# A vision tower's attention steps: both heads' scores issued together, and one row maximum for the two

## What is computed

```python
# xt: 257 rows of the image (normed) and 196 shared rows: 453 keys; 12 heads of width 16
qkv = (xt @ W_qkv).reshape(B, N1, 3, H, Dh)
attn = softmax(einsum('bhqd,bhkd->bhqk', q, k) * Dh ** -0.5)
out = einsum('bhqk,bhkd->bhqd', attn, v)[..., :257 rows]
h = h + out @ W_proj + b_proj
```

## Time and profile before

| | us |
|---|---|
| median of 3 runs | 716.21 (713.61 to 717.03) |
| the profiled execution | 714.55, with a span of 712.7 |
| TensorE busy in the span | 608.6 (85%) |
| VectorE | 281.4 (39%) |
| ScalarE | 202.5 (28%) |
| GpSimd | 144.8 (20%) |
| straight scores L660, 192 passes of 96 products | 62.5, mean 590 ns |
| maxima L879, 96 operations | 55.9, mean 623 ns |
| turned products L678, 384 passes | 65.9, mean 399 ns |
| exponentials L843, 48 operations | 49.1, mean 1024 ns |

### The profile page before, as it was taken

One profiled execution on the slowest core, in us unless ns is written; L12 is line 12 of the kernel. 1 busy time (PEld: TensorE's weight loads), 2 busy tenths in 40 slices (PEclk: granted clock), 3 DMA queues, 4 the chain that ended last, 5 costly groups with the idle time before them and its releaser, 6 DMA issues. The chain is left out here.

```text
span 712.7 us, 11088 instructions
## 1 busy us (share of the span) xinstructions
PE 608.6 (85%) x4373; PEld 440.0 (62%) x4382; DVE 281.4 (39%) x654; ACT 202.5 (28%) x481; POOL 144.8 (20%) x216
## 2 busy tenths in 40 slices
PE   2103979999999989888999999998887999989996
PEld 1002649555555543334899999988444556749995
DVE  0000042567767546995133333355362215302221
ACT  2001241154444414432633333400350001212220
POOL 6771110011111111442000000002006411232222
PEclk9999999999999999999999999999998999999999
DMA  8407141000000000501976777000722783166650
GB/s 220 146 5 281 52 126 42 1 1 1 2 1 1 2 1 0 157 23 39 360 311 266 272 289 293 12 1 1 271 81 56 242 331 168 38 218 185 192 179 1
DMA packets 27499, 86.75 MB, mean 122 GB/s; under 512 B 7822, under 2 KB 17351, under 8 KB 22330
## 3 DMA queue, kind: packets, MB, share of 16 engines
q1 hardware_dynamic: 24778, 82.89, 33.7%
q0 software_dynamic: 2672, 3.17, 1.6%
HBM read 79.68 MB, written 7.04 MB: 122 GB/s over the span
## 5 line engine op out<-in xcount | busy, mean ns | idle before, releaser
L1534 DVE TENSOR_TENSOR eo<-banks,b_rows 32x192 f32<-32x192 f32 x128 | 45.3, 354 | 91.6 <-PE banks L1484 71.0
L1515 ACT ACTIVATE hid<-banks,soft_b 128x128 f32<-128x128 f32 x192 | 51.2, 398 | 73.2 <-PE banks L1470 73.2
L879 DVE TENSOR_REDUCE nm<-banks 128x1 f32<-128x453 f32 x96 | 55.9, 623 | 31.6 <-PE banks L660 31.3
L1484 PE MATMUL banks<-soft_pair_w,hid 128*128 128x192 f32 x384 | 66.4, 330 | 1.4 <-issue 1.4
L678 PE MATMUL banks<-qa,kt 32*99 32x256 f32 (+1 forms) x384 | 65.9, 399 | 0.0
L843 ACT ACTIVATE pt<-banks 128x1024 f32<-128x1024 f32 (+1 forms) x48 | 49.1, 1024 | 57.1 <-PE banks L678 57.1
L660 PE MATMUL banks<-kt,qt 32*128 32x453 f32 x192 | 62.5, 590 | 2.3 <-DVE nm L879 0.9
L1484 PEld LDWEIGHTS banks<-soft_pair_w,hid 128*128 128x128 f32 x384 | 62.0, 190 | 3.3 <-issue 1.6
L84 PE MATMUL banks<-dense 128*128 128x512 bf16 x159 | 41.9, 400 | 7.6 <-PEq L2515 5.8
L1465 PE MATMUL banks<-slots_a,soft_pair_w 128*128 128x128 f32 x384 | 45.9, 276 | 1.2 <-PEq L1180 1.1
L1465 PEld LDWEIGHTS banks<-slots_a,soft_pair_w 128*128 128x128 f32 x384 | 44.9, 192 | 2.4 <-issue 2.0
(11 more groups left out here) (292 smaller groups left out, 1011.6 us busy)
## 6 DMA issues: line engine op xcount, KB each, us to landing
soft_pair_w<-in_spair SPq DMA_DIRECT2D x32, 1152.0 KB, 7.4
hy_band<-in_hband SPq DMA_DIRECT2D x6, 1540.0 KB, 6.5
route_tile_wi<-in_wi SPq DMA_DIRECT2D x15, 576.0 KB
switch_wo<-in_wo SPq DMA_DIRECT2D x1, 4608.0 KB, 16.4
hy_x_spread<-x_rows SPq DMA_DIRECT2D x24, 128.5 KB, 5.1
sorted_x<-blank_rows SPq DMA_DIRECT2D x15, 193.0 KB
route_tile_x<-sorted_x SPq DMA_DIRECT2D x15, 193.0 KB
vt<-in_vt SPq DMA_DIRECT2D x1, 2496.0 KB
```

What stands on the lines that cost most here:

```text
L879: dve.tensor_reduce(nm[:, n % 2, j, at:at + 1], ps[:, q, 0:NK], AXX, ALU.max, negate=True).then_inc(maxed, 1)
L1484: mm = pe.matmul(ps[:, 6 + q, 0:D], hid[:, p % 2, q, j, :], w[:, at:at + D], start=j == 0, stop=j == HJ - 1)
L1515: ins = act.activation(hid[:, p % 2, q, j, :], hidden(p, q, j), ACT.Gelu, bias=k.b1[:, 2 * p + q, j:j + 1])
L1534: dve.tensor_tensor(eo[SL * r:SL * (r + 1), b, i, :], ps[SL * b:SL * (b + 1), 6 + e % 2, 0:D], b2[SL * r:SL * (r + 1), i, :], ALU.add).the ...
```

## The change

A pair's two scores become one unit. `scores(m)` issues both heads, waits once for `maxed` (one count for a pair) and counts `score` once, on the second. `both_scores` issues it ahead of all four turned products, which then follow without anything between them. `negmax` waits once and takes the maximum of both banks in one TENSOR_REDUCE, which writes two columns of `nm`, 32 apart. `max_rows` waits for half the count. Ahead of the loop each pair of calls for q = 0 and 1 becomes one call. The number of products, their shapes and banks stay as they are.

```diff
-                def scores(m, q):
+                def scores(m):
                     n, i = m // 4, m % 4
-                    b, c, j, g = n // HC, n % HC, i // 2, i % 2 * 2 + q
+                    b, c, j = n // HC, n % HC, i // 2
                     if m >= 1:
-                        pe.wait_ge(maxed, 2 * (m - 1) + q + 1)
-                    row = slice(QUAD * g, QUAD * (g + 1))
-                    pe.matmul(ps[:, q, 0:NK], qt[row, c, b, j * P:(j + 1) * P], kt[row, c, b, :],
-                              start=True, stop=True).then_inc(score, 1)
+                        pe.wait_ge(maxed, m)
+                    for q in range(2):
+                        g = i % 2 * 2 + q
+                        row = slice(QUAD * g, QUAD * (g + 1))
+                        mm = pe.matmul(ps[:, q, 0:NK], qt[row, c, b, j * P:(j + 1) * P], kt[row, c, b, :],
+                                       start=True, stop=True)
+                    mm.then_inc(score, 1)
 
                 def max_rows(n):
-                    pe.wait_ge(maxed, 8 * n + 8)
+                    pe.wait_ge(maxed, 4 * n + 4)
...
                 def both_scores(n, i):
                     s = 4 * n + i
-                    ahead = s + 5
-                    if ahead < 4 * CHUNKS:
-                        scores(ahead, 0)
+                    if s + 5 < 4 * CHUNKS:
+                        scores(s + 5)
                     if i == 0:
                         pe.wait_ge(qa_r, n + 1)
                     if s >= 2:
                         pe.wait_ge(exped, s - 1)
-                    scores_t(n, i, 0, 0)
-                    if ahead < 4 * CHUNKS:
-                        scores(ahead, 1)
-                    scores_t(n, i, 0, 1)
-                    scores_t(n, i, 1, 0)
-                    scores_t(n, i, 1, 1).then_inc(scored_t, 1)
+                    for u in range(2):
+                        for q in range(2):
+                            mm = scores_t(n, i, u, q)
+                    mm.then_inc(scored_t, 1)
...
-                    for q in range(2):
-                        dve.wait_ge(score, 2 * m + q + 1)
-                        at = QUAD * (2 * p + q) + DH
-                        dve.tensor_reduce(nm[:, n % 2, j, at:at + 1], ps[:, q, 0:NK], AXX, ALU.max,
-                                          negate=True).then_inc(maxed, 1)
+                    dve.wait_ge(score, m + 1)
+                    at = QUAD * 2 * p + DH
+                    dve.tensor_reduce(nm[:, n % 2, j, at:at + QUAD + 1:QUAD], ps[:, 0:2, 0:NK], AXX, ALU.max,
+                                      negate=True).then_inc(maxed, 1)
```

More of the change, by code:

```diff
@@ L736, in _ @@
                 pe.wait_ge(k_r, HC * LAST)
-                for q in range(2):
-                    scores(0, q)
+                scores(0)
                 q_product(LAST, 0, 2)
                 q_product(LAST, 1, 3)
-                for q in range(2):
-                    scores(1, q)
+                scores(1)
                 q_product(LAST, 2, 4)
                 k_product(LAST, 0, 5)
-                for q in range(2):
-                    scores(2, q)
+                scores(2)
                 pe.wait_ge(q_r, HC * LAST + 2)
@@ L749, in _ @@
                 k_product(LAST, 2, 3)
-                for q in range(2):
-                    scores(3, q)
+                scores(3)
                 pe.wait_ge(q_r, HC * B)
@@ L766, in _ @@
                 max_rows(0)
-                for q in range(2):
-                    scores(4, q)
+                scores(4)
                 pe.wait_ge(v_r, B)
```

## The result

The changed kernel takes 728.1 us (median of 6 runs, 727.2 to 732.1) against 715.2 beside it; the ratio is 1.0166 (95% interval 1.0131 to 1.0201). In two later comparisons it was 1.0181 (1.0128 to 1.0235) and 1.0140 (1.0104 to 1.0176). It is slower by 10 to 13 us, where the forecast was a loss of 8.3 us and a time of 724.0.

The account below looks back on a forecast made before the run. TensorE and VectorE wait for each other, three limits taking turns over 42 periods; the terms sum to +8.3 us, taking 714.55 to 722.9 (724.5 from the median run). Forecast 724.0, range 719.5 to 728.5.

Parts of the forecast that it names:

- Joint maximum of 1.10 us, from a line through two rows: VectorE's one maximum over 906 columns: 1096 ns from rows of 453 and 1024 columns, against 1.17 us for two.
- The estimate from "VectorE: DVE Perf Modes" in the Trainium skill: PSUM operation of 120 cycles plus one per column at 0.96 GHz: 1.07 us joint, 1.16 for two, saving 0.10.
- The loop of 2.28: Score to joint maximum to next score in ordinary attention steps: 1.13 + 1.10 + 0.06 = 2.28 us, against 1.81.
- The joint duration stands in 40 periods, and decides at 0.89 us: Joint maximum counts in all periods but three with projection, plus the last pair; below 0.89 us the change gains.
- The projection, 3.77: Three i = 0 periods with a projection fall from 4.32 to 3.77 us, -1.65 in all.
- TensorE's own path falls to that of 203.95: With both scores ahead of the turned products, TensorE alone needs 1.62 us, hidden except where a projection follows the values.
- Other periods: 2.92 us ahead of the row of maxima, 2.40 with statistics of the next norm, 2.21 for the first two.
- rival D: TensorE idle some 0.6 us each step lowers its clock: at most 1 us a period, up to 764; chance 0.03.
- The reason for the low chance of D: The trace before has such TensorE pauses in 51 places and shows no swing of the clock.
- A: Joint maximum faster than its columns: at 0.62 us the loop is 1.81 again, 705 us; chance with E 0.05.
- E: Only the order of the scores acts: 2.17 becomes 1.62 in seven i = 0 periods; chance with A 0.05.
- Rival C's shorter way: Series partly hidden: maximum starts at +1.06, or shorter way from maximum to score; 719 with a low run; chance 0.07.

Follow-up runs that it names:

- The run at 0.893: Changed kernel with the joint maximum reading only the last 352 columns of each bank, 704 in all: 719.6 us, 1.0028 of before.
- the third profile of the changed kernel: The changed kernel unaltered, run again beside the one with filling products: 729.9 us (before 719.8), ratio 1.0140; its 42 periods take 108.3 us.
- the two filled ones: Changed kernel plus two dense filling products behind the values of i = 0 and 1, no projection near: 727.8 us (1.0114 of before), then 731.0 (1.0158).

## Why the prediction was right, and where it was short

The direction, the mechanism and the place were right, and the time lay in the range (719.5 to 728.5), but only 0.4 us below its upper end, and two of the six executions lie above it. That it lies inside is in part luck: the range took over a spread of 713.6 to 717.0 from three runs of before, and of the six beside the changed kernel one took 724.7. By the steps of the prediction:

- *Joint maximum of 1.10 us, from a line through two rows*: measured 1103 ns, with 630 and 893 at the two other sizes. The line gave 1096, 622 and 885, 7 or 8 ns low throughout. The estimate from "VectorE: DVE Perf Modes" in the Trainium skill was 1.07, and the trace sides with the rows. (For two separate maxima the same formula gives an estimate of 1.19, not the prediction's 1.16, and a saving of 0.12; nothing in the forecast uses it.)
- *The loop of 2.28*: 2.30 to 2.31. The way from the first score to the maximum is 1.15, not 1.13, probably since the second head's score is now the one waited for. With the 7 ns that is 0.02 in 27 periods, 0.5 us.
- *The joint duration stands in 40 periods, and decides at 0.89 us*: 39 among the 42 periods, and the last pair's makes the fortieth, as counted (from it to the last product of L718 it is 18.32, 18.11 and 17.85 us at the three durations). The run at 0.893 came out 0.3% above before, within what can be told from no change. Its steps are 1.7 us longer than those of before, so by them the sign changes at an estimated 0.85 us (1.103 - 9.9/39); the 0.04 comes from the other terms being too small.
- *The projection, 3.77*: 3.89. The step that failed is "TensorE's own path falls to that of 203.95": that row is of a step i = 3, and at i = 0 one wait more stands ahead of the turned products. It costs 0.1 us, hidden everywhere but here; 0.4 us in all.
- *Other periods*: 2.94 to 2.95 instead of 2.92 ahead of the row of maxima, 0.2 us in all; 2.39 to 2.40 with statistics, as forecast, and 2.23 instead of 2.21 for the first two. One maximum, at the same place in every profile with 48 maxima and the row of maxima ahead of the scores, starts 0.36 us late (period 2.66, i = 3 of chunk 8) without a wait to explain it; this was not foreseen and its cause stays open. One thing goes with it: in each of these nine profiles a transfer of 8 KB on the instruction queue (q14) starts 0.66 to 0.93 us behind that maximum's start, at 230.85 in the third profile of the changed kernel. The kernel before has such a transfer too, at 206.20, and no late maximum there. So the loading of VectorE's code is a candidate that no run here tested.
- Together the steps cost 9.9 us instead of 8.3. Of the 1.6 between them 0.5, 0.4 and 0.2 are sizes of terms that the sum has, 0.36 is the late maximum, which it has not, and the rest is rounding and the first two.
- *The clock* (rival D, 0.03, priced only as a fall throughout): one stretch of 7 us in one of three profiles, 1.9 us. It was a term, not a case, and its price was about right: the two periods in it grew by 0.86 and 1.07, where at most 1 was reckoned.
- *The reason for the low chance of D* did not hold: the 51 times of the earlier trace rows are waits of the weight loads, and the products themselves waited for a maximum 3 times, 0.9 us in all, against 28 times and 17.5 us after. So no row of before had shown that pauses like the new ones leave the clock alone. Their part in it is not settled. Such a stretch lies among the steps in three of the eight profiles with a joint maximum and no filling (the first, that with the old order, and that with the waits first), in neither of the two filled ones and in none of the four with two maxima. That leans towards the change, but is too little to show it. For the rule of the Trainium skill on pauses between groups of matmuls ("TensorE: Matmul & The Clock Gate", psum-queue depth-cycling) this case has pauses of 0.5 to 0.7 us in nearly every step, a swing in some profiles, and no measured gain from filling half of them.
- *Rivals A and E*: the joint maximum of half the columns came out 9 to 10 us below before, where A reckoned 11, which shows A's mechanism to be real and only its premise false. E is refuted by the order alone. Rival C's shorter way did not come: 1.15 stood where 1.13 had.
- The medians of the three comparisons are 12.9, 10.3 and 10.1 us apart. The steps account for 10 of each; the 1.4% that this makes lies inside all three intervals, and what is above it can't be told from the spread of the later stages.

## To carry over

Before two small operations are made one, ask which of them a loop waits for. Two maxima in 1.17 us cost the loop only the first's 0.62, and the joint one costs all of its 1.10 to save 0.07 of VectorE's time, of which there was enough. Multiply the loop's growth by the number of turns in which nothing else is longer, and the price comes out before anything is built. Here each bank is a single buffer between the two engines, so one count for both heads put the two scores and the whole joint maximum in series; whether a second pair of banks would take that away was not tested.

## What was not expected

- Two waits in a row between products cost 0.1 us here: turned products start at +0.11 where two waits stand, at +0.01 where there is one.
- The lower clock comes in stretches of 3 to 10 us at much the same places of the later stages in every kernel, but their lengths differ from one execution to the next. The later stages of the changed kernel differ by 5 us with it, and whole executions are best compared at the same clock in these stages.
- A low mean clock may cost little: in the profile of the order alone it is 0.944, since the clock is low for 58 us from 20 us on, when TensorE is busy for 17 of 59 us, and its time is 716.3, below the 718.2 of its median.
